# Layer 1 of a two-layer gated cross-attention: four heads' scores in two halves, out of phase

## The reference

```python
def _L0_xattn_ref(x_query, x_context, Wq, Wkv, Wp, bp, ln_g, ln_b):
    q = (x_query @ Wq).reshape(B, Nq, H, D).transpose(0, 2, 1, 3)
    kv = (x_context @ Wkv).reshape(B, Nc, 2, H, D)
    k = kv[:, :, 0].transpose(0, 2, 1, 3)
    v = kv[:, :, 1].transpose(0, 2, 1, 3)
    q = layernorm(q, ln_g, ln_b)
    k = layernorm(k, ln_g, ln_b)
    q = q * SCALE
    attn = jnp.einsum('bhqd,bhkd->bhqk', q, k)
    attn = jax.nn.softmax(attn, axis=-1)
    out = jnp.einsum('bhqk,bhkd->bhqd', attn, v)
    return out.transpose(0, 2, 1, 3).reshape(B, Nq, H * D) @ Wp + bp
...
x = x + jnp.tanh(g_xattn[0]) * _L0_xattn_ref(_layernorm(x, axis=-1), ctx_1024, ...)
x = x + jnp.tanh(g_ffn[0]) * _L0_ffn_ref(...)
x = x + jnp.tanh(g_xattn[1]) * _L1_xattn_ref(...)
x = x + jnp.tanh(g_ffn[1]) * _L1_ffn_ref(...)
```

## Time and profile before

| | |
|---|---|
| median of 3 runs | 569.25 us (569.05 to 570.59) |
| the profiled execution | 569.69 us, of which the profile's span is 567.9 us |
| TensorE (PE) busy | 545.3 us, 96% |
| its weight loads (PEld) | 470.8 us, 83% |
| VectorE (DVE) busy | 392.3 us, 69% |
| ScalarE (ACT) busy | 318.7 us, 56% |
| GpSimd (POOL) busy | 224.6 us, 40% |
| the four scores of a quad (L651, 256 matmul records) | 28.8 us |
| the turned scores (L669, 768 records) | 29.5 us |
| maximum (L1285, 32) | 55.0 us |
| Exp (L1824, 32) | 41.4 us |

### The profile page before, as it was taken

One profiled execution on the slowest core, in us unless ns is written; L12 is line 12 of the kernel. 1 busy time (PEld: TensorE's weight loads), 2 busy tenths in 40 slices (PEclk: granted clock), 3 DMA queues, 4 the chain that ended last, 5 costly groups with the idle time before them and its releaser, 6 DMA issues.

```text
span 567.9 us, 13539 instructions
## 1 busy us (share of the span) xinstructions
PE 545.3 (96%) x5530; PEld 470.8 (83%) x5530; DVE 392.3 (69%) x764; ACT 318.7 (56%) x629; POOL 224.6 (40%) x239
## 2 busy tenths in 40 slices
PE   8999999999999999999999999999799998999994
PEld 8776767777767878988898888888799996999994
DVE  7887477687778757668765756667576774677752
ACT  2454545565556566665656665557456574567631
POOL 2568549568560124235233432412311333132432
PEclk9999999999999999999999999999999999999998
DMA  8920680000000000000000000007581577077111
GB/s 245 358 75 2 231 330 3 1 3 1 2 2 2 1 1 2 2 9 26 2 26 10 17 17 10 26 1 306 214 273 62 205 261 249 21 255 264 19 13 23
DMA packets 22971, 50.66 MB, mean 89 GB/s; under 512 B 6464, under 2 KB 15728, under 8 KB 19568
## 3 DMA queue, kind: packets, MB, share of 16 engines
q1 hardware_dynamic: 18208, 44.94, 21.9%
q0 software_dynamic: 3456, 3.69, 3.5%
q10 hardware_dynamic: 1232, 1.01, 0.6%
HBM read 37.63 MB, written 12.52 MB: 88 GB/s over the span
## 4 chain that ended last, share of the span: by engine, by line
PE 80%; POOL 9%; DVE 6%; issue 3%; ACT 1%; DMA 1%; POOLq 0%
PE ps L65 16%; PE ps L67 15%; PE ps L66 15%; POOL sr L2087 6%; PE ps L794 5%; PE ps L812 5%; PE ps L782 5%; PE ps L651 4%; PE ps L669 3%; DVE KN L1285 3%; PE ps L685 2%; PE ps L630 2%; PE ps L559 1%; PE ps L910 1%; PE ps L588 1%
## 5 line engine op out<-in xcount | busy, mean ns | idle before, releaser
L2087 POOL TENSOR_TENSOR sr<-sv,mhalf 125x32 f32<-125x32 f32 x13 | 70.6, 5434 | 1.1
L65 PE MATMUL ps<-XGf,WH 128*128 128x256 f32 x252 | 71.0, 282 | 0.0
L66 PE MATMUL ps<-XGf,WH 128*128 128x256 f32 x252 | 71.0, 282 | 0.0
L67 PE MATMUL ps<-XGf,WL 128*128 128x256 f32 x252 | 70.7, 281 | 0.0
L1285 DVE TENSOR_REDUCE KN<-ps 112x4 f32<-112x1500 f32 x32 | 55.0, 1719 | 18.6 <-PE ps L651 18.3
L1700 DVE TENSOR_TENSOR WL<-WR,WH 128x1024 fp32r<-128x1024 f32 x48 | 57.1, 1220 | 12.7 <-ACT WH L2044 8.5
L2160 POOL TENSOR_SCALAR P<-P,rinv 112x487 f32<-112x487 f32 x56 | 40.7, 738 | 55.3 <-DVE rinv L1328 55.0
L1889 ACT ACTIVATE P<-ps,nm 112x487 f32<-112x487 f32 x64 | 41.9, 664 | 23.6 <-DVE nm L1320 23.6
L1824 ACT ACTIVATE P<-ps 125x1344 f32<-125x1344 f32 x32 | 41.4, 1293 | 22.7 <-PE ps L669 22.2
L464 POOL DMA_INDIRECT out<-WS,rows_i x16 | 28.7, 1796 | 62.5 <-ACT WS L1978 47.0
L2044 ACT ACTIVATE WH<-WR 128x1024 fp32r<-128x1024 f32 x48 | 48.7, 1050 | 0.1
(11 more groups left out here) (302 smaller groups left out, 1505.0 us busy)
## 6 DMA issues: line engine op xcount, KB each, us to landing
WR<-in_gupT SPq DMA_DIRECT2D x16, 1024.0 KB, 7.6
WR<-in_dwnT SPq DMA_DIRECT2D x8, 1024.0 KB, 10.8
xs<-ZT SPq DMA_DIRECT2D x14, 516.0 KB, 6.7
CT<-in_ctxT SPq DMA_DIRECT2D x1, 2250.0 KB, 10.5
P<-xs SPq DMA_DIRECT2D x7, 256.0 KB, 10.1
Wk<-in_L_xattn_Wk SPq DMA_DIRECT2D x2, 512.0 KB, 11.4
Wv<-in_L_xattn_Wv SPq DMA_DIRECT2D x2, 512.0 KB, 11.8
out<-X SPq DMA_DIRECT2D x8, 112.0 KB, 1.9
```

Of the source, the lines that this page charges most:

```text
L65: e.matmul(out, ah, bh, start=start, stop=False)
L66: e.matmul(out, ah, bl, start=False, stop=False)
L67: return e.matmul(out, al, bh, start=False, stop=stop)
L2087: e.tensor_tensor(sr[:, p, :], sv[:, p, :], mhalf[0:125, 0:32], ALU.pow).then_inc(s("sr"), 1)
```

## The change

The four heads of a quad are treated as two halves, (q, 0) with heads 0 and 1 and (q, 1) with heads 2 and 3. A step `S0` q h now issues the scores of two heads of quad q and, in the other two banks, the turned scores of two heads of an earlier quad: heads 2 and 3 of q - 2 beside (q, 0), heads 0 and 1 of q - 1 beside (q, 1). The stage `st` is gone. `max0` and `ex` are split into halves as well, of 750 and 672 columns. Three further steps, (32, 0), (32, 1) and (33, 0), carry the last turned scores alone; (0, 0), (0, 1) and (1, 0) have scores alone. `ex` and `V0` get later offsets, the stages behind layer 1's values (TAIL0) and the start of layer 2 (T1) too, and some transposes and copies are moved.

```diff
-QUAD = ((-0.89, 'S0'), (0.21, 'max0'), (4.39, 'qt2'), (5.19, 'qt2c'), (7.76, 'st'), (9.14, 'ex'), (10.19, 'V0'))
+QUAD = ((-0.89, 'S0', 0), (0.21, 'max0', 0), (1.6, 'S0', 1), (2.7, 'max0', 1), (4.39, 'qt2'), (5.19, 'qt2c'),
+        (8.3, 'ex', 0), (11.31, 'ex', 1), (12.65, 'V0'))
...
-TAIL0 = ((27.84, 'ob'), (31.17, 'obT'), (31.05, 'aw'), (33.66, 'awT'), (33.1, 'aT'), (45.62, 'wo'),
...
+TAIL0 = ((31.24, 'ob'), (34.57, 'obT'), (34.45, 'aw'), (36.45, 'awT'), (36.9, 'aT'), (49.02, 'wo'),
...
-    T1 = TQ * NQUAD + 4
+    T1 = TQ * NQUAD + 6.3
...
+    for q, h in ((NQUAD, 0), (NQUAD, 1), (NQUAD + 1, 0)):
+        at(TQ * q + QUAD[2 * h][0], "S0", q, h)
...
+        def turned_scores(e, q, g, j):
+
+            b, k = divmod(q, 4)
+            rows = slice(32 * g, 32 * g + 32)
+            return e.matmul(ps[0:125, g, j * NQ:(j + 1) * NQ], KT[b % 2][rows, k, j * 125:(j + 1) * 125],
+                            QB[b % 2][rows, k * NQ:(k + 1) * NQ], start=True, stop=True, tile_position=(32 * g, 0))
...
+                    r = q - 1 if h else q - 2
+                    tops = [2 * h, 2 * h + 1] if q < NQUAD else []
+                    turned = [2 - 2 * h, 3 - 2 * h] if r >= 0 else []
+                    if tops:
+                        b, k = divmod(q, 4)
+                        if q >= 2:
+                            w.wait_ge(s("ex"), 2 * (q - 2) + h + 1)
...
+                    if turned:
+                        w.wait_ge(s("smax"), min(2 * q + h, 2 * NQUAD))
+                        for sem_, v in emptied(("qt2", r)):
                             w.wait_ge(sem_, v)
...
+                    for j in range(3):
+                        for g in turned:
+                            t = turned_scores(e, r, g, j)
+                        if turned and j == 2:
+                            t.then_inc(s("st"), 1)
+                        if j == 0:
+                            for g in tops:
+                                rows = slice(32 * g, 32 * g + 32)
+                                t = e.matmul(ps[0:NQ, g, 0:NC], QA[b % 2][rows, k * NQ:(k + 1) * NQ],
+                                             KT[b % 2][rows, k, 0:NC], start=True, stop=True, tile_position=(32 * g, 0))
+                            if tops:
+                                t.then_inc(s("sc0"), 1)
```

More of the change, by code:

```diff
@@ L209, in attention_order @@
     for q in range(NQUAD):
-        for d, stage in QUAD:
-            at(TQ * q + d, stage, q)
+        for d, stage, *h in QUAD:
+            at(TQ * q + d, stage, q, *h)
+    for q, h in ((NQUAD, 0), (NQUAD, 1), (NQUAD + 1, 0)):
+        at(TQ * q + QUAD[2 * h][0], "S0", q, h)
     pair_at = [T1 + TP * p if p < NPAIR - 4 else T1 + TP * (NPAIR - 4) + TL * (p - NPAIR + 4) for p in range(NPAIR)]
@@ L641, in tensor_attention @@
                 elif stage == "S0":
[L642 to L647, removed]
-                            w.wait_ge(sem_, v)
[L649 to L653, removed]
+                    q, h = i
+                    r = q - 1 if h else q - 2
[5 more added lines that the diff above has]
+                            w.wait_ge(s("ex"), 2 * (q - 2) + h + 1)
+                        if k == 0:
+                            for sem_, v in emptied(*(("spk", b, j) for j in range(3)), ("spq", b)):
+                                w.wait_ge(sem_, v)
+                    if turned:
+                        w.wait_ge(s("smax"), min(2 * q + h, 2 * NQUAD))
+                        for sem_, v in emptied(("qt2", r)):
+                            w.wait_ge(sem_, v)
+                    for j in range(3):
[10 more added lines that the diff above has]
+                                t.then_inc(s("sc0"), 1)
                 elif stage == "qt2":
@@ L657, in tensor_attention @@
                     bk = take(stage, q)
-                    w.wait_ge(s("smax"), q + 1)
+                    w.wait_ge(s("smax"), 2 * q + 2)
                     e.transpose(ps[:, bk, 0:NQ], KN[b % 2][0:NQ, 3, k * 128:(k + 1) * 128],
                                 ident[0:NQ, 0:NQ]).then_inc(s("qt2"), 1)
[L661 to L672, removed]
                 elif stage == "V0":
@@ L759, in tensor_attention @@
                     if p == 0:
-                        w.wait_ge(s("smax"), NQUAD)
-                        w.wait_ge(s("ex"), NQUAD)
+                        w.wait_ge(s("smax"), 2 * NQUAD)
+                        w.wait_ge(s("ex"), 2 * NQUAD)
                     products = [("k1", b, f)]
@@ L1281, in vector_attention @@
                 elif stage == "max0":
-                    q, = i
+                    q, h = i
                     b, k = divmod(q, 4)
-                    w.wait_ge(s("sc0"), q + 1)
-                    e.tensor_reduce(heads(KN[b % 2][0:NQ, 3, :])[:, 4 * k:4 * k + 4, 16], ps[0:NQ, 0:4, 0:NC], AX.X,
+                    w.wait_ge(s("sc0"), 2 * q + h + 1)
+                    first = 4 * k + 2 * h
+                    e.tensor_reduce(heads(KN[b % 2][0:NQ, 3, :])[:, first:first + 2, 16], ps[0:NQ, 2 * h:2 * h + 2, 0:NC], AX.X,
                                     ALU.max, negate=True).then_inc(s("smax"), 1)
@@ L1505, in keys_copy @@
             if b >= 2:
-                w.wait_ge(s("sc0"), 4 * (b - 1))
-                w.wait_ge(s("st"), 4 * (b - 1))
+                w.wait_ge(s("sc0"), 8 * (b - 1))
+                w.wait_ge(s("st"), 8 * (b - 1))
             dst = KT[b % 2][:, :, j * 125:(j + 1) * 125]
@@ L1819, in scalar_attention @@
                 elif stage == "ex":
-                    q, = i
-                    w.wait_ge(s("st"), q + 1)
+                    q, h = i
+                    w.wait_ge(s("st"), 2 * q + h + 1)
                     if q >= 3:
                         w.wait_ge(s("av0"), q - 2)
-                    e.activation(PQ[:, q % 3, :].rearrange("p (g n) -> p g n", g=4), ps[0:125, 0:4, 0:3 * NQ],
+                    hs = slice(2 * h, 2 * h + 2)
+                    e.activation(PQ[:, q % 3, :].rearrange("p (g n) -> p g n", g=4)[:, hs, :], ps[0:125, hs, 0:3 * NQ],
                                  ACT.Exp).then_inc(s("ex"), 1)
```

28 lines of the change are left out of this document (14 added, 14 removed).

## The result

The changed kernel takes 618.44 us (median of 4; 569.22 before): a ratio of 1.0835, 95% interval 1.0786 to 1.0884. The forecast was slower, 586.5 with a range of 571 to 600: the sign was right, the size was short by 32 us. The profiled execution took 614.69 (span 612.9); the two longest, near 620.7, had a mean granted TensorE clock of 0.972 where this one has 0.980.

The account below looks back on a forecast made before the run. TensorE's queue was taken as the bound of layer 1. Full batches 9.6, light batches 2.8, quads 25 to 28 1.6 and the end 3.3 made 17.3 us on 569.69: 587.0, median 586.5, range 571 to 600.

Parts of the forecast that it names:

- first rival: Chance 15%: TensorE's waits simply go, if at least 1.95 us of work stand between all half-steps; 566.5 us.
- Stalls 1 and 3: TensorE waits 1.2 us from 20.0 to 20.1, and 1.0 us from 17.0 to the query transposes behind 18.0.
- the walk: The prediction's pass through the engines' queues over one batch, half-steps 17.0 to 21.0, to find TensorE's waits.
- Stall 2: From 19.0 to 19.1 TensorE waits 1.3 us, as quad 17's half Exp stands behind other work on ScalarE.
- products not named cost what their rows show: Assumption for the batch from 17.0 to 21.0: TensorE products not discussed keep their profiled cost.
- Sum 3.5 us in a full batch: TensorE's three forecast waits together, giving +3.2 us for each of the three batches of quads 13 to 24.
- The light batches: Quads 5 to 12, which lack the residual and the tanh on VectorE and ScalarE: +1.4 us, twice.
- I take half a full batch, 1.6 (bounds 0 and 3.2). The end: 2.5 and one stall like the first, 0.8: Quads 25 to 28, no keys left to prepare: +1.6 us; layer 1's end: extra steps 2.5 and a wait 0.8.
- a sign that its walk is wrong: The prediction's own test: its queue reading is wrong if the loss lies at the end rather than in quads 13 to 24.
- the start, forecast at 0: Start of layer 1, taken as held by the inverse root on GpSimd, 5.4 us at a time: 0 us added.

Follow-up runs that it names:

- e1: Changed kernel with the output transposes obT moved from behind the query transposes spq to ahead of a token transpose; 610.57 us, ratio 1.0713.
- e2: Changed kernel with one value product moved from behind half-step 20.1 to ahead of it, likewise in each batch from the third on; 617.72 us, ratio 1.0843.
- e5: Changed kernel with 51 other offsets, so that 0.8 to 1.7 us of other TensorE work stand between any two half-steps; 575.98 us, ratio 1.0119.
- e7: Kernel before the change, with ScalarE repeating the Exp of quad 13 once, 18 twice and 23 four times; 580.98 us, ratio 1.0192.
- e4: Changed kernel with 124 useless identity transposes put into TensorE's waits of quads 12 to 28; 615.41 us, ratio 1.0832.
- e8: e5 with the last batch's four query transposes placed one half-step and one feed-forward product later in TensorE's queue; 575.81 us, ratio 1.0104.

## Why the prediction was right and wrong

*Right: the sign, and the pieces.* The half maximum, the half Exp and the mixed half-step cost what was drawn from the rows of before (934 ns, 730 ns and 0.84 us). The first rival's condition, 1.95 us of work between all half-steps, fails at 20.0 to 20.1, as argued. The half Exp ahead of the turned scores heads the list of waits, as forecast; the half maximum, forecast ahead of the turned scores too, stands in the second line instead, ahead of qt2. TensorE's busy share is 18.94 of 22, 86% where 87% was forecast; that it comes so near is in part luck of the window, for over the batch from 119.60 to 146.11 it is 22.21 of 26.51, 84%.

*Stalls 1 and 3 were right in size.* The wait ahead of 20.1 is 149.81 less 148.33 less 0.18 for the transposes, 1.3 us (forecast 1.2), and the half Exp does stand behind XT. The query transpose of quad 17 waits 1.1 us for a KT copy that came late on VectorE (forecast 1.0 in two places). The transposes spq, at which the walk put the end of that stall, do not wait in this batch.

*Stall 2 was too large, for a reason that made the sum too small.* It measures 0.4 (forecast 1.3; these sizes are from a product's start to the next one's, less what it costs without a wait, so a little above the idle time in brackets): TensorE came 0.8 us later to that place, because it had waited just ahead. The walk took "products not named cost what their rows show". Four places on that path did not: obT behind spq, whose copy QA still reads the bank (0.8); qt2 of quad 18 behind the copy from awT (0.6); the key products behind the half-step 19.0, whose bank kraw still reads (0.2); and qt2 of quad 20 behind the half maximum (1.0). These rows of the changed kernel show three of them:

```profile
136.44 0.65 PE L846 MATMUL ps<-ident,S 128*112 128x128 f32 x4 [0.64 <-ACT QA L1825]
...
141.55 0.32 PE L685 MATMUL ps<-ident,KN 112*128 112x112 f32 x1 [0.51 <-ACT S L1921]
...
151.58 0.69 DVE L1289 TENSOR_TENSOR KN<-kraw,sr 125x512 f32<-125x512 f32 x1 [2.20 <-POOL sr L2103]
...
152.19 0.93 DVE L1300 TENSOR_REDUCE KN<-ps 112x2 f32<-112x750 f32 x1
...
153.18 0.32 PE L685 MATMUL ps<-ident,KN 112*128 112x112 f32 x1 [0.83 <-DVE KN L1300]
```

The last three rows belong together. The half maximum of 20.1 could have begun at 150.8, 0.95 behind its half-step as at 20.0, and have been ready at 151.7, when TensorE was not yet there (152.2). It began 1.4 later, because on VectorE it stands behind the KN scaling, and that waited 2.20 for the inverse root (146.11 to 151.55). The walk had a scaling in stall 3 alone, and no wait of VectorE for a root. The first step that failed is **"Sum 3.5 us in a full batch"**: the waits are 5.4 (1.3, 0.4, 1.1, 0.8, 0.6, 0.2 and 1.0), which less the 0.35 of before makes a batch some 5 us longer; 4.8 were measured (5.9 in the third of the three), 3.2 forecast. The walk had followed the banks of the scores; banks 5 to 7 have the same rule, and VectorE's order can hold a half maximum back. e1 shows one such place on the chip, e2 that the waits hang together in a chain, and e5 that another order has none of them.

*The light batches* were forecast 1.4 longer each and came out 2.4 and 3.2 longer (68.15 less 43.19 against 63.95 less 41.37, 93.01 less 68.15 against 85.63 less 63.95).

*The end and the clock were the larger miss.* The second step that failed is **"I take half a full batch, 1.6 (bounds 0 and 3.2). The end: 2.5 and one stall like the first, 0.8"**. Behind the root at 150.75 that makes 4.9; 22.1 were measured. The three full batches lost 15.5 (9.6 forecast), so the larger part lies at the end, which the prediction had itself named as a sign that its walk is wrong. 2.5 are the three extra steps, at their forecast price (0.84 each from start to next). 9.4 are waits of the same kinds: between 173.66 and 245.74 TensorE is idle for 11.0 us, before between 150.75 and 204.90 for 1.6 (1.0 us up to 188.2, 1.75 up to 206.0 and 1.8 up to 224.3 are among the 11.0). At most 7.7 are the clock, for which the prediction had no term and no rival. Some 2.5 are left, which these events do not place. Windows of the changed kernel:

```profile
186.00:188.00 2.00, 0.96 (x8) 0.66 (x6) 1.41 (x3) 0.88 (x3) 0.77 (x2) 1.00 0.00 0
...
190.00:195.00 5.00, 4.68 (x49) 3.83 (x49) 2.53 (x4) 2.01 (x3) 0.18 (x1) 0.50 0.00 0
...
203.00:206.00 3.00, 1.25 (x11) 1.04 (x11) 2.93 (x8) 0.12 (x1) 2.38 (x4) 0.97 0.00 0
206.00:216.00 10.00, 8.93 (x83) 7.17 (x84) 4.13 (x6) 4.46 (x9) 0.07 (x1) 0.50 0.00 0
```

From 188.7 to 195.6 and from 205.8 to 216.0 TensorE ran at its lower level, each time behind a stretch in which it had been idle for more than half; some 15 busy us there would take half at the upper level. The clock had fallen once before, from 28.3 to 31.7, behind a wait of 2.30 us at a query transpose (timeline and window):

```profile
26.87 0.32 PE L685 MATMUL ps<-ident,KN 112*128 112x112 f32 x1 [2.30 <-DVE KN L1300]
...
28.00:32.00 4.00, 4.00 (x23) 2.91 (x24) 2.63 (x3) 2.22 (x4) 3.29 (x3) 0.57 0.84 287
```

That is at most 1.7 us; the start, forecast at 0, came out 1.8 longer. In the changed kernel itself this cost is only worked out. That waits bring such falls, and that these cost time, is seen in e7, in the kernel before; e4 tried to show it in the changed kernel and did not.

*The gain that the change could have had* was small: 5.6 us of waits in the whole stage, less 2.5 for the extra steps. e5 has 1.4 us of such waits left (38 to 206 us) and is 2.1 us ahead of before at the root of 150.75; with the extra steps and the clock behind that it is still 1.2% slower.

## What to carry to other kernels

Read first what the bounding engine still waits in the stage, here 5.6 us: no shorter loop can give back more, and any new order can lose far more. Splitting a step in two doubles the places at which a queue must not come too early, so go through every product between two halves, and ask of each bank, not of the split ones alone, which copy empties it and what stands ahead of that copy; here a half maximum stood behind a scaling that waited for a root of 5.4 us. And allow for it that a wait of one to a few microseconds on TensorE costs more than its length: in these runs some were followed by a fall of the clock.

## What the hardware showed beyond that

The clock did not follow single waits in a way that these runs explain. The same wait had a fall behind it in one run and none in another: 1.96 us in e8 but not 1.95 in e5, and 1.99 in e7 but not 1.94 in the kernel before. The clock fell behind 2.20 us in e7 and behind 2.30 in the changed kernel, but not behind 2.13 in e2 (up to 179.96; the next fall came 9 us later, behind another wait). It stayed up behind 1.30 us in e7 and behind the waits of 1.1 us in each full batch of the changed kernel; yet in e5 it fell 6.7 us behind a wait of 0.71, with none above 0.15 in between, and stayed low for 6.8. What it answers to there is open. And in e5 a batch with almost no wait took as long as one with 0.35 us of waits. Some products cost more in that order: the four query products (L615) cost 1.05 us from start to next where the order of before (L605) had 0.77, and the changed kernel too (145.64 to 146.40). In e5 V0 follows them, in the other two a key product. Why that should matter was not tried.
